# Four chained blocks on one core: queries and keys in three buffers in turn, low parts written over them, and an earlier transposition on VectorE

## What is computed

```python
x = L0(x, cond, ctx, masks)   # adaLN; attention with rotary q and k and a mask (l0);
                              # attention to 77 context tokens with a mask (l0c); gated MLP
x = L1(x, cond, ctx)          # softmax over prototypes, router over 3 experts, gate
x = L2(x, ctx, cond)          # attention to the 77 context tokens (l2)
x = L3(x, ctx, cond)          # self-attention (l3s), attention to the context (l3c), FFN

def attention(q, k, v, mask):
    s = einsum('bqhd,bkhd->bhqk', q, k) * 8 ** -0.5
    return einsum('bhqk,bkhd->bqhd', softmax(where(mask, s, min)), v)
```

## Time and profile before

| | |
|---|---|
| runs | 1174.65, 1185.07, 1185.32 us; median 1185.07 |
| the profiled execution's own time | 1176.95 us |
| span of its trace | 1174.8 us |
| around the span | 2.15 us |
| mean granted clock | 0.856 of full |

### The profile page before, as it was taken

The page is one execution under the profiler, slowest core; times in us unless marked ns, Lnnn a source line. Parts: engine busy times, 40 slices in busy tenths (PEclk is TensorE's granted clock), DMA queues, the critical chain, the costliest instruction groups (busy, mean ns, idle before and its releaser), DMA issues.

```text
span 1174.8 us, 32004 instructions
## 1 busy us (share of the span) xinstructions
PE 1074.7 (91%) x12961; PEld 725.9 (62%) x12961; DVE 744.3 (63%) x1852; ACT 622.1 (53%) x938; POOL 618.1 (53%) x739
## 2 busy tenths in 40 slices
PE   7898899989998999999999999889888988897998
PEld 5455555656666676676666566656555655565676
DVE  7757856767666443777778566767777754565521
ACT  2134434565656655454455455655556765654653
POOL 6657757665565432112226567665577553465531
PEclk9669968988777999999999667887889987876899
DMA  6423322332232102000000323232332323222101
GB/s 233 146 70 111 126 83 83 125 124 90 84 118 82 46 28 90 10 7 6 11 12 30 103 70 111 84 98 95 118 123 96 118 89 114 83 80 72 59 28 45
DMA packets 101459, 96.89 MB, mean 82 GB/s; under 512 B 11632, under 2 KB 93808, under 8 KB 100928
## 3 DMA queue, kind: packets, MB, share of 16 engines
q1 hardware_dynamic: 101312, 94.84, 24.3%
HBM read 18.77 MB, written 2.15 MB: 18 GB/s over the span
## 4 chain that ended last, share of the span: by engine, by line
PE 60%; POOL 12%; SPq 9%; issue 8%; DVE 6%; DMA 2%; ACT 2%; POOLq 0%; ACTq 0%; DVEq 0%
PE weighed L725 11%; PE scores L896 6%; PE row_scores L658 5%; PE weighed L748 5%; SPq L2135 4%; SPq L2138 4%; PE scores L695 4%; PE scores L613 3%; PE scores L710 3%; DVE negmax L1217 3%; PE row_scores L896 3%; PE quads L620 2%; POOL kblk_r L1927 2%; DMA q_ring<-qr 2%; PE quads L605 2%
## 5 line engine op out<-in xcount | busy, mean ns | idle before, releaser
L1217 DVE TENSOR_REDUCE negmax<-row_scores 128x8 f32<-128x616 f32 (+1 forms) x312 | 299.9, 961 | 248.7 <-PE row_scores L658 203.2
L1733 ACT ACTIVATE p<-scores 128x1024 f32<-128x1024 f32 (+1 forms) x253 | 251.6, 1019 | 145.3 <-PE scores L710 141.0
L1927 POOL TENSOR_TENSOR kblk_r<-work,pack_const 128x308 fp32r<-128x308 f32 (+1 forms) x160 | 133.9, 838 | 197.3 <-PE row_scores L658 183.2
L725 PE MATMUL weighed<-p,v 77*32 77x128 f32 (+1 forms) x5120 | 213.9, 319 | 2.1 <-DVE nat L1233 1.3
L725 PEld LDWEIGHTS weighed<-p,v 77*32 77x32 f32 (+1 forms) x5120 | 157.4, 127 | 57.9 <-issue 45.1
L658 PE MATMUL row_scores<-kblk_r,qr 32*128 32x308 f32 (+1 forms) x624 | 161.0, 511 | 16.6 <-DVE negmax L1217 13.4
L695 PE MATMUL scores<-q_ring,k_ring 32*77 32x128 f32 (+1 forms) x2512 | 136.4, 284 | 39.4 <-ACT p L1733 31.2
L695 PEld LDWEIGHTS scores<-q_ring,k_ring 32*77 32x77 f32 (+1 forms) x2512 | 112.1, 194 | 48.0 <-ACT p L1733 35.9
L658 PEld LDWEIGHTS row_scores<-kblk_r,qr 32*128 32x128 f32 x624 | 68.5, 214 | 104.1 <-DVE negmax L1217 49.9
L710 PE MATMUL scores<-nblk,select 32*77 32x512 bf16 (+1 forms) x628 | 104.2, 463 | 0.0
L1970 POOL TENSOR_TENSOR attn<-nat,rden 128x128 f32<-128x128 f32 x160 | 65.0, 406 | 61.5 <-DVE rden L1238 61.1
(11 more groups left out here) (334 smaller groups left out, 2027.4 us busy)
## 6 DMA issues: line engine op xcount, KB each, us to landing
q_ring<-work SPq DMA_DIRECT2D x160, 128.0 KB, 2.1
q_ring<-qr SPq DMA_DIRECT2D x160, 128.0 KB, 2.1
k_ring<-k_high SPq DMA_DIRECT2D x64, 128.0 KB, 2.1
k_ring<-work SPq DMA_DIRECT2D x64, 128.0 KB, 2.1
k_ring<-k_high SPq DMA_DIRECT2D x96, 77.0 KB, 2.0
k_ring<-work SPq DMA_DIRECT2D x96, 77.0 KB, 2.0
shared<-gates_hbm SPq DMA_DIRECT2D x24, 256.0 KB, 3.2
shared<-in_ctx_tok SPq DMA_DIRECT2D x15, 154.0 KB
```

What stands on the lines that cost most here:

```text
L725: mm = e.matmul(av_bank[TILE * j:TILE * j + TILE, i2 * S:(i2 + 1) * S], v[0:nk, at:at + TILE], p[n % 2][0:nk, g * NJ + j, :], start=i1 == ...
L1217: e.tensor_reduce(negmax[q % 2][:, 2 * h:2 * h + 2, s * NJ:(s + 1) * NJ], row_banks(n, h)[:, :, 0:NJ * nk].rearrange("p g (j k) -> p g j k ...
L1733: e.activation(p[n % 2][0:nk, 8 * h:8 * h + 8, :], score_banks(n, h)[0:nk].rearrange("p g (j q) -> p (g j) q", j=NJ), ACT.Exp, bias=hide, ...
L1927: e.tensor_tensor(kblk_r[n % 2][:, 0:NJ * nk].rearrange("p (j k) -> p j k", j=NJ), k_of[q % 2][:, s * nk:(s + 1) * nk].unsqueeze(1).to_bro ...
```

## The change

`q_of` and `k_of` get three buffers each in the same nine slices of `work`, `k_high` two. The low parts have no buffers: `split_q` and `split_k` write over `q_of` and `k_of`. A new `stacked(w, q)` waits until both pairs of quad q have landed. Rounding the keys of quad q waits for quad q-2 in place of q-1; writing new queries or keys of quad q waits for quad q-3; the splits wait for no landing, but `split_k` now for the four `spread_k` of its quad. At a phase's start `split_k` stands one slot later. On VectorE `turn_blocks(t-1)` stands ahead of `row_max(t+6, 0)`, and `turn_max` on TensorE waits for it.

```diff
@@ buffers
-        xn, q_of, k_of = [work[:, j, :] for j in range(3)], [work[:, 3 + j, :] for j in range(2)], [work[:, 6 + j, :] for j in range(2)]
-        q_low, k_low = work[:, 5, :], work[:, 8, :]
-        k_high = sb("k_high", [128, QUAD * S], F32R)
+        xn, q_of, k_of = ([work[:, 3 * i + j, :] for j in range(3)] for i in range(3))
+        k_high = [sb(f"k_high{i}", [128, QUAD * S], F32R) for i in range(2)]
+        def stacked(w, q):
+
+            for m in (2 * q, 2 * q + 1):
+                if m >= 0:
+                    w.wait_ge(*pair_landed(m))
@@ TensorE, turn_max(q)
+                if q:
+                    w.wait_ge(nat_done, 4 * q - (2 if layer_of(q - 1).mask == "qk" else 1))
@@ VectorE, rotate(q, which); take_q likewise
-                w.wait_ge(*freed)
-                if which:
-                    w.wait_ge(kblk_r_done, 4 * (q - 2) + 4)
+                stacked(w, q - 3)
@@ VectorE, attention
+                    if t - 1 in jobs:
+                        turn_blocks(t - 1)
                     if t + 6 in jobs:
                         row_max(t + 6, 0)
...
-                    if masked and cl == 2 and qi + 1 in quads:
-                        w.wait_ge(negmax_turned, qi + 2)
-                    if t - 1 in jobs:
-                        turn_blocks(t - 1)
                     if masked and cl == 2 and qi + 1 in quads:
                         spread_max(qi + 1)
@@ ScalarE, round_k(q)
-                w.wait_ge(k_split, q)
-                if q:
-                    w.wait_ge(*pair_landed(2 * q - 2))
-                    w.wait_ge(*pair_landed(2 * q - 1))
-                e.copy(k_high[:, 0:cols], k_of[q % 2][:, 0:cols]).then_inc(k_rounded, 1)
+                w.wait_ge(k_split, q - 1)
+                stacked(w, q - 2)
+                e.copy(k_high[q % 2][:, 0:cols], k_of[q % 3][:, 0:cols]).then_inc(k_rounded, 1)
@@ ScalarE, take_k(q); take_q likewise
-                w.wait_ge(k_split, q - 1)
-                w.wait_ge(kblk_r_done, 4 * (q - 2) + 4)
+                stacked(w, q - 3)
@@ GpSimd, split_q(q) and split_k(q)
-                if q:
-                    w.wait_ge(*pair_landed(2 * q - 2))
-                    w.wait_ge(*pair_landed(2 * q - 1))
-                e.tensor_tensor(q_low, q_of[q % 2], qr[q % 3][:, :].bitcast(F32), ALU.subtract).then_inc(q_split, 1)
+                e.tensor_tensor(q_of[q % 3], q_of[q % 3], qr[q % 3][:, :].bitcast(F32), ALU.subtract).then_inc(q_split, 1)
...
-                if q:
-                    w.wait_ge(*pair_landed(2 * q - 2))
-                    w.wait_ge(*pair_landed(2 * q - 1))
-                e.tensor_tensor(k_low[:, 0:cols], k_of[q % 2][:, 0:cols], k_high[:, 0:cols].bitcast(F32),
+                w.wait_ge(kblk_r_done, 4 * q + 4)
+                e.tensor_tensor(k_of[q % 3][:, 0:cols], k_of[q % 3][:, 0:cols], k_high[q % 2][:, 0:cols].bitcast(F32),
                                 ALU.subtract).then_inc(k_split, 1)
@@ GpSimd, attention
                     if t == 4 * lo - 5:
                         split_q(lo)
-                        split_k(lo)
-                    if cl == 0 and qi + 1 in quads and qi + 1 != lo:
-                        split_q(qi + 1)
+                    if cl == 0 and qi + 1 in quads:
+                        if qi + 1 != lo:
+                            split_q(qi + 1)
                         split_k(qi + 1)
```

31 lines of the change are left out of this document (15 added, 16 removed).

## The result

| | before | changed |
|---|---|---|
| median of the runs | 1185.19 us (4 runs, 1174.65 to 1186.49) | 1085.76 us (4 runs, 1074.11 to 1094.94) |
| profiled execution, its own time | 1176.95 us | 1094.94 us |
| span of its trace | 1174.8 us | 1093.1 us |
| mean granted clock | 0.856 | 0.906 |

The ratio of the changed kernel to the one before is 0.9146, 95% interval 0.9045 to 0.9247. Predicted were 1098 us for the median and 1094 for the profiled execution.

What follows compares the result with a forecast made beforehand. ScalarE's key roundings waiting for transfers were taken to stop TensorE and lower its clock. 98 us from five stages, less 5 (transposition) and 10 (`xh`), gave 83 off 1176.95: 1094, or 1098 as median; range 1055 to 1150.

Steps and rivals of the forecast that it cites:

- I count no wait: Scores in l3c: transfers of their own pair land in time, with only about 1.4 us of margin left.
- Rival B: Scores wait for their own first pair's landing; 49 of the 83 us lost, 1147 us; chance 0.12.
- The stages: Five attention stretches less reference quads: gains 25.4 (l3s), 29.8 (l3c), 7.9 (l2), 21.9 (l0c), 13 (l0), sum 98 us.
- Rival A: GpSimd's `xh` comes late in every quad that has it, with a low clock each time; 1118 us; chance 0.14.
- Rival C: Moved transposition lies on the loop in every slot, 64 us, and short stops keep the clock down; 1210 us; chance 0.04.
- 13 us for l0: Gain in l0's five quads at 21.3 us each: 14.8 us, reduced for the lower clock to 13.
- five more quads that pay 2 us each: GpSimd's `xh` becomes the late one in more quads once landing waits go: 10 us taken off the gain.
- 2 us off for the lower clock that such a stop can bring: In l0, allowance for low clock after the stop at L572, taking the gain from 14.8 to 13 us.
- 5 us of loss: VectorE's moved transposition delays first maxima, 0.5 us a quad over 19 narrow quads: 5 to 9 us, 5 taken.
- below 0.1 us in 39 places, nothing counted: `turn_max` on TensorE waits for `nat`, with two rows matmuls between: negligible, no time charged.
- the 152 us of that working: Skill's clock rule: 243 us of low time worth 121 us, plus 31 us of stops; weighed against 98, not adopted.
- Rival D: The clock comes back wholly, also at L572: 17 us more in l2, some 10 at phase starts; 1068 us; chance 0.08.

Runs made afterwards that it cites:

- round_k_waits: Changed kernel in which only the rounding of the keys waits again for quad q-1's pairs: 1194.64 us.
- before_xh_first: Kernel before with GpSimd's splits of slot cl = 0 moved behind `normalise_x`: 1222.48 us, ratio 1.0382.
- xh_first: Changed kernel with GpSimd's splits of slot cl = 0 moved behind `normalise_x`: 1046.79 us, ratio 0.8893.
- xh_first_filled: Changed kernel with splits behind `normalise_x`, transposition in its old place, and five filler matmuls ahead of `turn_normed` in a few quads: 1044.72 us, ratio 0.8847.
- late_nat: Changed kernel with VectorE's transposition back behind the first half's maxima and `turn_max` without its new wait: 1081.54 us, ratio 0.9116.
- early_nat_only: Kernel before with only VectorE's transposition moved early, buffers and landing waits as before: 1190.68 us, ratio 1.0044.
- after_again: The changed kernel itself, unaltered, run again as control against the kernel before: 1078.27 us, ratio 0.904.

## Why the prediction was right

**What bounds it.** The prediction read a chain: low parts, 11 us of issues, landing, rounding, exponential, scores. round_k_waits puts back one link and gets the whole time back. before_xh_first moves the low parts 2.1 us later within the whole chain and finds the rounding 2.4 us later in a like quad. Both show the chain by a change of time, not only by the trace.

**What is late next.** "I count no wait" for the landing of a quad's own pair was right for the changed kernel: no scores matmul waits for a transfer. Rival B is out. But the margin is as narrow as the prediction said. Where the low parts start some 2 us later, in xh_first, one quad waits 0.97 us, and in xh_first_filled four wait 1.8 us together.

**The stages.** The method was to multiply the quads that showed no stop in the trace of before. It gave 130.4 and 104.3 us for l3s and l3c, and they took 128.9 and 104.4. Rival A needed 8 x 18.3 = 146 us in l3s. Its first half came true, more stops at L572's place (22 for 16), but not its second, a low clock each time. Rival C needed the clock kept down, and l3s has 1.00. The 104.3 for l3c was in part luck, since two terms offset each other. The reference at a clock of 0.93 was too slow, 14.9 where a clean quad takes 14.0. Against that the last quad of the stage took 18.4 us, at the low clock behind a stop for the maxima that the prediction had not counted:

```profile
989.94 0.41 PE L663 MATMUL row_scores<-kblk_r,qr 32*128 32x308 f32 x2 [0.92 <-DVE negmax L1222]
```

**The step that was mis-sized: `xh` in l0.** The prediction set 13 us for l0 and, over all stages, 10 us for "five more quads that pay 2 us each". In l0 four of the five quads have a stop of 1.4 us and three of these weigh at the low clock behind it (24.1, 24.1 and 25.6 us, as read between first weighings); the other one begins at the low clock that it has from the phase's start (23.8 us). Together 119.1 us in place of 108.3. So l0 alone missed by 10.8 us, l0c and l2 by 3.2 and 3.1: together 17 us, against the 10 set aside. "2 us off for the lower clock that such a stop can bring" was the wrong size. Against the 21.4 us of the quad with a stop and no slow weighing, the three lost 9.6 us to the low clock, and the quad at the start 2.4 more that have nothing to do with `xh`. The 21.3 us that the prediction took for a quad with its stop was right. xh_first gives 106.0 us for the same five quads, 13.1 less, of which 3.2 are in that first quad.

**The transposition.** 5 us of loss were forecast, as 0.1 to 0.3 us a slot of later maxima. The place was wrong: the rows' wait for the maxima did not grow into a new stop, but `turn_max` waits 0.33 us for `nat`, 10.7 us in 28 places, where the prediction had "below 0.1 us in 39 places, nothing counted". It had counted two rows matmuls as cover and not that `nat` and its signal take 0.6 us against their 0.4. The net effect is too small for these runs: late_nat has 0.4 us less a quad in l3c and yet a median 3 us higher, early_nat_only is 3 us above before. Whether 5 us was the right size stays open.

**The clock.** The five stretches lost 243 us of low clock before. After, by the clock column, (1 - 0.86)/0.5 x 119.1 = 33 us, 18, 44, 0 and 8, together 103. For the 140 us less, TensorE's busy time in them fell from 572.0 to 512.8, 59 us: 0.42 us for each. The Trainium skill (TensorE: Matmul & The Clock Gate, Terms) would price the 140 us at a half, 70. The measurement decides, 59, which is not far off. What made the 152 us of that working wrong was mainly that 103 us of low clock stayed. Rival D, with the clock wholly back, is not this kernel, but xh_first at 1046.8 shows that its 1068 was within reach, and more. (By its own terms, 17 and 10 us off 1098, D comes to 1071.)

**The time.** The sum said 83 us off the profiled execution, which is 82.0 shorter. That it is so near is partly luck: the changed kernel's profiled execution is the slowest of its four runs, and its medians lie 99 us (four runs) and 109 us (after_again) below before's. The half of the scatter that was added, 4 us, went the wrong way. The mechanism holds without this match, and the number is in the forecast's range either way.

## What to carry to other kernels

When a queue's head waits for a transfer of the item before, look at what is queued behind it: one wait on ScalarE cost some 110 us here, through exponentials that had nothing to do with it, and more buffers for three small tiles removed it. A loop's own undisturbed iterations in the trace gave the time after the cut to about 1% in two stages of five, one of them by errors that offset; the three with the next-late stop came out 3 to 10% longer. So count that stop in every iteration that has it, with the low clock behind it. And once the chain is cut, try again the orders that it dictated: the same reordering on GpSimd cost 28 us before the change and gained 31 after it.

## What the runs showed of the hardware

- A stop of 1.43 us of TensorE was followed by a weighing at 1.94 us in place of 1.08, and a quad of l0 with it had 24.1 us at a granted clock of 0.86. Another quad of the same layer with a stop of 1.4 us at the same line took 21.4 us, without a slow weighing. In l3s stops of 0.5 to 0.7 us a quad left the clock at 1.00 throughout, but in l3c a weighing at 1.94 us came behind a stop of 0.92 us. So the length of a stop alone does not tell whether the clock falls.
- A low clock can last without any stop. The first quad of the second phase ran its 23.1 us in the changed kernel at 0.50 with TensorE busy nearly all the time (the row at 639.70), and the same quad 14.2 us at 1.00 in xh_first (the row at 615.70), with the same matmuls. TensorE was busy 22.87 us of the one and 12.85 us of the other, so at the low clock it had hardly any idle time left. What decides which of the two an execution gets was not settled; it may be much of the 12 to 32 us between runs of one kernel. The two kernels with fillers had the smallest such spread, 11.9 and 11.7 us.
- Fillers that did no useful work took 22 us off the changed kernel's median (some 4 us by the ratios), though they cost 0.4 us a quad where the clock was up.
- Taking a stop away can gain only the clock. In l0 a quad of xh_first takes 21.4 us without the stop for `xh`, and so did a quad of the changed kernel with the stop of 1.44 us at the full clock.
